# Attention in a two-layer block: sums merged in place, maxima sent straight to the stack, projections two positions earlier

## What is computed

```python
q = _heads(x @ Wq + bq)
att = jnp.where(causal[None, None], jnp.einsum('bhqd,bhkd->bhqk', q, k) * scale, -jnp.inf)
y = jnp.einsum('bhqk,bhkd->bhqd', jax.nn.softmax(att, axis=-1), v)
y = y + jnp.einsum('bhqk,bhkd->bhqd', jax.nn.softmax(attc, axis=-1), vc)
...
return y @ Wp + bp
...
x = x + jnp.tanh(g_xattn[0]) * _L0_xattn_ref(_layernorm(x, axis=-1), ctx_512, ...)
x = x + jnp.tanh(g_ffn[0]) * _L0_ffn_ref(_layernorm(x, axis=-1), ...)
```

## Time and profile before

| | us |
|---|---|
| median of 3 runs | 1790.24 |
| lowest, highest | 1783.11, 1794.31 |
| profiled execution, whole time | 1790.51 |
| its span in the profile | 1788.8 |
| PE busy | 1520.2 (85%) |
| DVE busy | 1145.0 (64%) |
| POOL busy | 903.8 (51%) |
| ACT busy | 853.1 (48%) |
| mean granted PE clock | 0.914 |

### The profile page before, as it was taken

The page is one execution under the profiler, slowest core; times in us unless marked ns, Lnnn a source line. Parts: engine busy times, 40 slices in busy tenths (PEclk is TensorE's granted clock), DMA queues, the critical chain, the costliest instruction groups (busy, mean ns, idle before and its releaser), DMA issues. The chain is left out here.

```text
span 1788.8 us, 34467 instructions
## 1 busy us (share of the span) xinstructions
PE 1520.2 (85%) x10516; PEld 922.2 (52%) x10579; DVE 1145.0 (64%) x2869; ACT 853.1 (48%) x1823; POOL 903.8 (51%) x1497
## 2 busy tenths in 40 slices
PE   4897988989798888989898988989647988888786
PEld 2454544445454444445454545445314777777564
DVE  5666666767667666667667667667514555655698
ACT  3464645546455645545555545555330322322445
POOL 2253445464645456364645555464533454665674
PEclk8998879999898989888898889999887999999999
DMA  6775747677675757576675757676583565444697
GB/s 163 191 198 141 214 146 201 194 187 206 184 205 171 210 173 200 169 200 179 190 212 165 217 159 190 192 204 195 180 233 111 168 212 187 143 148 136 214 309 248
DMA packets 218015, 337.42 MB, mean 189 GB/s; under 512 B 44072, under 2 KB 147248, under 8 KB 217840
## 3 DMA queue, kind: packets, MB, share of 16 engines
q1 hardware_dynamic: 168048, 230.95, 48.1%
q10 hardware_dynamic: 36832, 67.80, 11.0%
q0 software_dynamic: 12960, 36.51, 5.8%
HBM read 193.84 MB, written 140.27 MB: 187 GB/s over the span
## 5 line engine op out<-in xcount | busy, mean ns | idle before, releaser
L1264 DVE TENSOR_REDUCE nmax<-vector_bank 128x1 f32<-128x384 f32 (+4 forms) x832 | 514.8, 640 | 212.7 <-PE vector_bank L1450 196.8
L928 ACT ACTIVATE pt<-scalar_bank 128x512 f32<-128x512 f32 x640 | 352.0, 603 | 371.8 <-PE scalar_bank L1413 365.9
L744 POOL TENSOR_SCALAR_AFFINE_SELECT pt<-pt 128x256 f32<-128x256 f32 (+1 forms) x640 | 223.7, 362 | 246.4 <-ACT pt L928 236.0
L1413 PE MATMUL scalar_bank<-stack 99*64 99x512 bf16 (+4 forms) x1280 | 309.3, 349 | 17.7 <-ACT ct L928 5.0
L1450 PE MATMUL vector_bank<-stack 96*128 96x128 bf16 (+3 forms) x1024 | 263.4, 320 | 4.8 <-issue 1.6
L1768 POOL DMA_INDIRECT rows<-pt x142 | 137.8, 971 | 125.6 <-DVE pt L1894 81.8
L1402 PE MATMUL scalar_bank<-xnT,w_qk 128*128 128x512 f32 x384 | 183.9, 603 | 10.1 <-ACT xnT L842 10.1
L1476 PE MATMUL pv_self<-pt,vst 128*32 128x512 f32 (+3 forms) x2048 | 183.3, 487 | 4.1 <-ACT usum L883 4.1
L1447 PE MATMUL vector_bank<-tri,ident_b 128*128 128x128 bf16 (+2 forms) x641 | 157.6, 246 | 18.8 <-DMA stack<-qk_scratch 10.6
L703 POOL DMA_INDIRECT rows<-xn,slot x128 | 140.9, 1101 | 59.5 <-issue 31.4
L1413 PEld LDWEIGHTS scalar_bank<-stack 99*128 99x128 bf16 (+1 forms) x1280 | 109.7, 108 | 111.8 <-issue 47.8
(11 more groups left out here) (299 smaller groups left out, 2506.1 us busy)
## 6 DMA issues: line engine op xcount, KB each, us to landing
qk_scratch<-parts SPq DMA_DIRECT2D x31, 1200.0 KB, 4.6
sum_scratch<-usum ACTq DMA_DIRECT2D x64, 512.0 KB, 4.0
stack<-qk_scratch SPq DMA_DIRECT2D x120, 192.0 KB, 3.1
pt<-rows SPq DMA_DIRECT2D x142, 132.0 KB
stack<-qk_scratch SPq DMA_DIRECT2D x248, 72.0 KB, 2.8
packed<-sum_scratch SPq DMA_DIRECT2D x32, 512.0 KB
inverse<-inverse_scratch SPq DMA_DIRECT2D x32, 512.0 KB, 5.0
pt<-rows SPq DMA_DIRECT2D x16, 1024.0 KB, 6.2
```

Source lines behind the costliest of these rows:

```text
L744: pool.affine_select(out=v, in_=v, compare_op=ALU.is_ge, fill=0.0, base=0, pattern=pat, channel_multiplier=-1).then_inc(masked, 1)
L928: act.activation(dst, bank(kind, ("st", c, k))[:, :], ACT.Exp, scale=SCALE).then_inc(scalar_drained, 1)
L1264: dve.tensor_reduce(dst, src, axis=AX, op=ALU.max, negate=True).then_inc(vector_drained, 1)
L1413: return pe.matmul(out, stack[c][0:rows, head, key0:key0 + nk], stack[c][0:rows, head, q0:q0 + nq], start=True, stop=True, **kw)
```

## The change

- `max_rows`: the transposed maxima are now ordered head by head, and four DMAs take them straight from `mT` to the stack, without the scratch and without a wait on SP between.
- The ones stand at place 15 for heads of group 1, with their values at places 16 to 31. ACT copies group 0 to `packed[c]` and group 1 to `late`; `merge` then moves the 16 result rows of the four heads of group 1 by four DMAs of 16 partitions into the same partitions of `packed[c]`, over the row of sums of group 0, which has been taken before. `wp` is loaded in the order that fits. The sum scratch, its stores and `read_packed` are gone.
- The sums are inverted, and the inverses stored, per group. In half 0 that is at (1, 3) and (1, 12), for (1, 13) before, and SP's first stack read of half 1 now comes behind the second store.
- The output projections move from positions 10 to 13 of half 0 to 8 to 11, and with them all that follows on the previous item by two positions; the multiplication for half 1 moves from position 7 to 6.
- Values and cross values are written by one instruction for each group.

```diff
-PREV_UNITS = {(0, 10): ("wp", 0), (0, 11): ("wp", 1), (0, 12): ("wp", 2), (0, 13): ("wp", 3),
-              (0, 22): ("rT", 0), (0, 23): ("rT", 1), (1, 0): ("rT", 2), (1, 1): ("rT", 3), (1, 2): ("rl",), (1, 16): ("rk",)}
-
-ROUTE_STEPS = {(0, 11): ("stats", 0), (0, 12): ("stats", 1), (0, 13): ("stats", 2), (0, 14): ("stats", 3), (0, 15): "aggregate",
-               (0, 19): "normalise", (1, 3): "max", (1, 4): "shift", (1, 6): "sum",
-               (1, 7): "invert", (1, 8): "probs", (1, 9): "top", (1, 10): "index", (1, 11): "as float",
-               (1, 12): "hot", (1, 13): "both", (1, 14): "weigh", (1, 17): "own rows", (1, 18): "at",
-               (1, 19): "slots", (1, 20): "keep"}
-ROUTE_EXP = (1, 5)
-SUMS_INVERTED = (1, 13)
-SUMS_SCALED = (0, 7)
+PREV_UNITS = {(0, 8): ("wp", 0), (0, 9): ("wp", 1), (0, 10): ("wp", 2), (0, 11): ("wp", 3),
+              (0, 20): ("rT", 0), (0, 21): ("rT", 1), (0, 22): ("rT", 2), (0, 23): ("rT", 3), (1, 0): ("rl",), (1, 14): ("rk",)}
+
+ROUTE_STEPS = {(0, 9): ("stats", 0), (0, 10): ("stats", 1), (0, 11): ("stats", 2), (0, 12): ("stats", 3), (0, 13): "aggregate",
+               (0, 17): "normalise", (1, 1): "max", (1, 2): "shift", (1, 4): "sum",
+               (1, 5): "invert", (1, 6): "probs", (1, 7): "top", (1, 8): "index", (1, 9): "as float",
+               (1, 10): "hot", (1, 11): "both", (1, 12): "weigh", (1, 15): "own rows", (1, 16): "at",
+               (1, 17): "slots", (1, 18): "keep"}
+ROUTE_EXP = (1, 3)
+FIRST_HALF_INVERTED = {0: (1, 3), 1: (1, 12)}
+SECOND_HALF_SCALED = (0, 6)
...
-        usum_all = sb("usum", [P, 4, T])
-        usum = {(w, g): usum_all[:, 2 * g + i, :] for i, w in enumerate(("x", "s")) for g in range(2)}
-        packed = sb("packed", [P, 2, T])
+        packed_all = sb("packed", [P, KC, 2, T])
+        packed = [packed_all[:, c, :, :] for c in range(KC)]
+        late = sb("late_sums", [P, 2, T])
...
-                heads = slice(HEAD_GROUP * g, HEAD_GROUP * (g + 1))
                 sp.wait_ge(vector_drained, VU.upto(kind, b, ("mT", c, g)))
-                sp.dma_start(mscr[c, g].rearrange("s (n t) -> (s n) t", t=P), mT[c][g][:, :]).then_inc(m_stored, 16)
-                sp.wait_ge(m_stored, 16 * MSPLIT.upto(kind, b, (c, g)))
-                sp.dma_start(stack[c][STACK:STACK + MROWS, heads, 0:K0],
-                             mscr[c, g].rearrange("s (h t) -> s h t", h=HEAD_GROUP)).then_inc(m_in[c][g], 16)
-
-            def read_packed(s, c):
+                n = MROWS * 2 * QT
+                for j in range(HEAD_GROUP):
+                    sp.dma_start(stack[c][STACK:STACK + MROWS, HEAD_GROUP * g + j, 0:K0],
+                                 mT[c][g][j * n:(j + 1) * n, :]).then_inc(m_in[c][g], 16)
+
+            def write_inverse(s, c, g):
 
                 n = normalised(s, c)
-                for g in range(2):
-                    sp.wait_ge(sums_stored[c][g], 16 * (s + 1))
-                if n > 1:
-                    sp.wait_ge(y_added, YADD.credit + n - 1)
-                rows = uscr[c].rearrange("g (j r) w t -> g j r (w t)", r=32)[:, :, 0:D, :]
-                sp.dma_start(packed[:, :, :].rearrange("p w t -> p (w t)"),
-                             rows.rearrange("g j d x -> d (g j) x")).then_inc(packed_in, 16)
-
-            def write_inverse(s, c):
-
-                n = normalised(s, c)
-                sp.wait_ge(sums_inverted, n)
+                sp.wait_ge(sums_inverted[g], n)
                 if n > 2:
                     sp.wait_ge(inverse_in, 16 * (n - 2))
-                sp.dma_start(iscr[c].rearrange("h w (k i) -> (h w k) i", i=SUM_RUN), sums[c][:, :]).then_inc(inverse_stored, 16)
+                sp.dma_start(iscr[c][:, g, :], sums[c][64 * g:64 * g + 64, :]).then_inc(inverse_stored, 16)
 
             def read_inverse(s, c):
 
                 n = normalised(s, c)
-                sp.wait_ge(inverse_stored, 16 * n)
+                sp.wait_ge(inverse_stored, 32 * n)
                 if n > 1:
                     sp.wait_ge(scaled, n - 1)
-                rows = iscr[c].rearrange("h w t -> h (w t)").unsqueeze(0).to_broadcast([D, HU, 2 * T])
+                rows = iscr[c].rearrange("j g x -> (j g) x").unsqueeze(1).to_broadcast([HU, D, 2 * T])
...
-                    write_inverse(b - 1, 1)
-                    read_packed(b - 1, 1)
+                    write_inverse(b - 1, 1, 1)
...
-                if cur and not nxt:
-                    write_inverse(b, 0)
-                    read_packed(b, 0)
-                    read_inverse(b, 0)
+                if cur:
+                    write_inverse(b, 0, 0)
+                    write_inverse(b, 0, 1)
+                    if not nxt:
+                        read_inverse(b, 0)
+                        write_inverse(b, 1, 0)
...
-                            if cur:
-                                read_inverse(b, 0)
                             max_rows(kind, b, 0, 0)
                         read_stack(kind, b, 1, pair)
                         if pair == 0 and cur:
-                            write_inverse(b, 0)
-                            read_packed(b, 0)
+                            read_inverse(b, 0)
+                    if cur:
+                        write_inverse(b, 1, 0)
...
-                if c == 1:
-                    act.wait_ge(sums_stored[0][g], 16 * (b + 1))
-                    act.wait_ge(sums_in[0], 32 * (b + 1))
-                elif b > 0:
-                    act.wait_ge(sums_stored[1][g], 16 * b)
-                    act.wait_ge(sums_in[1], 32 * b)
+                if g == 0:
+                    if b > 0:
+                        act.wait_ge(y_added, YADD.credit + normalised(b - 1, c))
+                    dst = packed[c]
+                else:
+                    before = 2 * b + c
+                    if before > 0:
+                        s, pc = divmod(before - 1, KC)
+                        act.wait_ge(merged[pc], 16 * HEAD_GROUP * (s + 1))
+                        act.wait_ge(sums_in[pc][1], 16 * (s + 1))
+                    dst = late
                 act.wait_ge(pv_filled, PV.upto(kind, b, (w, c, g)))
-                act.activation(usum[w, g][:, :], (pv_cross if w == "x" else pv_self)[:, :], ACT.Copy).then_inc(pv_drained, 1)
-
-            def store_sums(kind, b, c, g):
+                act.activation(dst[:, 0 if w == "x" else 1, :], (pv_cross if w == "x" else pv_self)[:, :],
+                               ACT.Copy).then_inc(pv_drained, 1)
+
+            def take_sums(kind, b, c, g):
 
                 act.wait_ge(pv_drained, PV.upto(kind, b, ("s", c, g)))
                 if b > 0:
-                    act.wait_ge(inverse_stored, 16 * normalised(b - 1, c))
-                act.dma_start(sums[c][64 * g:64 * g + 64, :], usum_all[D:P:32, 2 * g:2 * g + 2, :].rearrange("j w t -> j (w t)")
-                              ).then_inc(sums_in[c], 16)
-                if b > 0:
-                    act.wait_ge(packed_in, 16 * normalised(b - 1, c))
-                act.dma_start(uscr[c, g], usum_all[:, 2 * g:2 * g + 2, :]).then_inc(sums_stored[c][g], 16)
+                    act.wait_ge(inverse_stored, 32 * normalised(b - 1, c))
+                src = packed[c][D:P:32, :, :] if g == 0 else late[D - 1:P:32, :, :]
+                act.dma_start(sums[c][64 * g:64 * g + 64, :], src.rearrange("j w t -> j (w t)")).then_inc(sums_in[c][g], 16)
+
+            def merge(kind, b, c):
+
+                act.wait_ge(sums_in[c][0], 16 * (b + 1))
+                for j in range(HEAD_GROUP):
+                    rows = slice(32 * j + D, 32 * j + 2 * D)
+                    act.dma_start(packed[c][rows, :, :], late[rows, :, :]).then_inc(merged[c], 16)
...
-                            store_sums(kind, b, 0, 1)
+                            take_sums(kind, b, 0, 1)
+                            merge(kind, b, 0)
...
-                            store_sums(kind, b, 1, 0)
+                            take_sums(kind, b, 1, 0)
                             unnormalised(kind, b, "s", 1, 1)
-                            store_sums(kind, b, 1, 1)
+                            take_sums(kind, b, 1, 1)
+                            merge(kind, b, 1)
...
-                ps = filled(kind, b, ("v", c))
-                dve.tensor_tensor(vst[:, :, c, :, 0:D], ps[:, :].rearrange("p (t h d) -> p t h d", t=QT, d=D),
-                                  bv[:, c, :, :].rearrange("p t (h d) -> p t h d", d=D), ALU.add).then_inc(vector_drained, 1)
+                ps = filled(kind, b, ("v", c))[:, :].rearrange("p (t h d) -> p t h d", t=QT, d=D)
+                for g in range(2):
+                    heads = slice(HEAD_GROUP * g, HEAD_GROUP * (g + 1))
+                    last = dve.tensor_tensor(vst[:, :, c, heads, D * g:D * g + D], ps[:, :, heads, :],
+                                             bv[:, c, :, :].rearrange("p t (h d) -> p t h d", d=D)[:, :, heads, :], ALU.add)
+                last.then_inc(vector_drained, 1)
...
-            def invert_sums(s, c):
```

(8 more changed lines are left out.)

93 lines of the change are left out of this document (50 added, 43 removed).

## The result

The changed kernel takes 1878.7 us (median of 4 runs, 1874.7 to 1880.4), the kernel before 1791.2 beside it: a ratio of **1.049**, 95% interval 1.045 to 1.053. The forecast was 1755 us, with 1708 to 1803 as the range. On another chip, where the kernel before took 1782 us, the ratio was 1.054 (1.050 to 1.058). Its time lay between 1736 and 1791 us from one measurement to the next, and most of the difference lies behind the attention: from the start of the last output projection to the end the traces have 398 to 401 us where the kernel before took 1736 to 1742 us, and 436 to 444 us where it took 1776 to 1791. Two of these measurements (1776 and 1736 us) bear the same chip's number; what sets this part is open.

What follows compares the result with a forecast made beforehand. PE was taken to set the pace of the attention loop, through its waits, clock and instructions. The terms -20 -15 -7 +20 +13.5 -22 -4 gave -34.5 on 1790.5 us: forecast 1755 us, range 1708 to 1803.

Steps and rivals of the forecast that it cites:

- rival B: Stores of inverses: narrow ones served by only four DMA engines take 2.0 us more; 1797 us, chance 0.20.
- item 5: Merge on ACT: four issues of 0.46 us, twice per iteration; +20 us mid half 1, +13.5 at the iteration's end.
- Rival C: Merge issues on ACT cost 1.1 us each and make the kernel slower: 1835 us, chance 0.15.
- Rival A: Merge issues on ACT are hidden and the clock recovers further: 1711 us, chance 0.15.
- Item 1: Output projections two positions earlier, inverses by group: yT releases PE 2.65 us earlier, net 1.3 per iteration, -20 us.
- item 4: Maxima straight to the stack, without SP's wait for the scratch: costed at nothing by itself.
- Items 2 and 3: PE's wait before the transpose of half 1's maxima shrinks by 1.0 us, -15 us; the router's 0.4 us wait goes, -7.
- Item 6: DVE's eight more instructions per iteration: nothing, as DVE has idle time; without that cover up to 66 us.
- Item 7: PE's clock in the attention loop: a fifth of the half-rate cost goes as waits shrink, 1.5 us per iteration, -22 us.
- Item 8: End of the kernel, PE's 19.0 us wait after the last item: -4 us without the sum traffic.

Runs made afterwards that it cites:

- experiment 1: The changed kernel with both merges issued by SP, in front of the last store of inverses, and none by ACT: ratio 1.025 to the kernel before.
- experiment 9: The kernel before with the maxima sent straight to the stack by four transfers, without the scratch, and nothing else: ratio 0.984.
- experiment 8: The kernel before with its tables moved two positions earlier as in the change, sums, inverses and maxima as before: ratio 0.993.
- version 10: The kernel before with the tables two positions earlier and the maxima sent straight to the stack: ratio 0.967.
- experiment 6: The changed kernel with both merges issued by SP, behind the stores of the inverses and ahead of their read: ratio 1.036.
- experiment 7: The changed kernel with SP's merges behind the stores of the inverses, and these stored twice so their read has outermost dimension 16: ratio 1.040.
- 12: The changed kernel with the inverses' read in sixteens and ACT's merge of half 1 behind the next item's xnT rows: ratio 1.016.

## Why the prediction was wrong

Two steps failed, by about as much each. The changed kernel is 88 us over the kernel before, where 34.5 under it was forecast.

**The first step that failed is the list of parts itself: the new form of the inverses' read has no item.** `[HU, D, 2T]` stood in the diff where `[D, HU, 2T]` had been. I weighed the rule on outermost dimensions below 16 against the stores (rival B), where it did no harm (C fell to 2.5), and kept the read at the old 4.5 us. It takes 6.4 us in the iteration shown and 7.0 in the median. That costs 3.0% in the changed kernel, about 57 us, and 3.5 to 4.3% elsewhere.

**The second is item 5,** +33.5 us, which priced the merge as four issues of 0.46 us and gave it no wait of its own. With a wide read, merge and inverses by group cost 1.020 / 0.967 = 5.5%, about 95 us, some 60 us more than item 5 had. The issues are 0.63 each, and the middle of half 1 came as worked out (a wait of 1.24 near (1,13)). At the end of the iteration the issues stand behind ACT's wait for the landing of the sums, which I never followed: 3.3 us, with the first projections at 1.2 GHz behind it. PE's wait on xnT was to be 1.5 and was 5.0. Without the merges on ACT (experiment 1) the kernel is 2.3% faster (1.025 / 1.049). Rival C (1835 us) had the right place and sign for the wrong reason: it wants issues of 1.1 us, and their median is 0.61. Rival B would have shown as stores of over 4.5 us; they took 2.5 in the median. Rival A fell with PE's waits on ACT.

**Item 1** counted 1.4 us from SP's earlier store. That was right (B: 2.2 to 0.6, experiment 9: -1.6%); it comes from **item 4**, as the prediction says ("its worth is in 1"). It also started from a wait of 3.4 us, where all but one of the waits are 3.0. In the changed kernel D and A gave the gain back, and the wait stayed at 3.0.

**Items 2 and 3** came as forecast in their waits (1.34 us for 2.2; the router's wait gone); the -12 us of experiment 8 needed the clock too. **Item 6**, eight more instructions of DVE, shows no wait. **Item 7**: the clock stayed (0.914, 0.912). The spell behind the transpose's wait went, and a new one came behind the wait on xnT. Its gain is there where that wait is not: 0.940 in experiment 8 and 0.949 in 10. It does not need short waits everywhere, as experiment 8 has 4.9 us before each output projection. **Item 8** was to give 4 us and gave nothing: PE's wait for the last item was 21.6 us for 19.0, that for the item before it 8.0 for 9.0.

Where the 8.2% between version 10 (0.967) and the changed kernel (1.049) went, by the table, us per iteration: F 8.2, of it A 7.3 (ACT's wait and issues, the slow clock behind them), D 1.9, less 1.4 in C; G 2.2, of which the middle's waits on ACT are 1.3 (57.7 to 56.4 in experiments 1 and 6, which have the merge on SP) and 0.9 is open. None of the placements tried brought the merge under the kernel before: on ACT early and late, and on SP behind the stores, each with both reads, and on SP ahead of the stores with the narrow read. Open: SP ahead of the stores with the wide read, which was not run (if the two ratios multiplied, 1.025 x 0.970 = 0.994, an estimate; experiments 7 and 12 show that they need not), and a placement in which the maxima and POOL's low parts move too.

## What to carry to other kernels

Write down the shape of every transfer that the diff touches, the unchanged ones in a new layout too, and look for a DMA share that stands at a half while an engine waits for one transfer. Before pricing an instruction that is put in front of others, follow what it must wait for to its issue. When a wait shrinks and the time doesn't, measure the whole chain from one fixed point to the next: here it was one loop, and what left one wait came back in the next. And when a number comes out as forecast, look whether its waits did: in experiment 8 a longer wait and a better clock made up the forecast sum.

## Not expected of the hardware

- A broadcast read of 512 KB took 4.6 to 5.1 us from issue to use with an outermost dimension of 16 and 6.7 to 7.0 with 8 (medians of all kernels). While DVE stood for a narrow one, 0.51 to 0.54 of the engines were busy, at 120 to 145 GB/s.
- Four transfers of 16 partitions (64 KB each) within SBUF cost ACT 2.5 us of issuing; SP 2.5 (experiment 6) to 3.3 (experiment 1).
- A multiply of 1.23 us took 4.1 us in the mean beside a tensor operation of POOL (experiment 7).
- A wait of 2.2 us of PE was followed by a spell at 1.2 GHz in 13 of 14 iterations, one of 1.3 us at the same place by none (experiment 8).
- A small transfer landed 7.0 us after its issue behind a narrow read, 5.6 behind a wide one.
